# An f32 opening, later transfers of two key groups, and eight more probability chunks transposed by DMA, in an attention and routed feed-forward kernel

## The reference

```python
xn = layernorm(x)
q = xn @ W_qk                                   # keys are xn itself
scores = q @ xn.T / 16 + slope * (kpos - qpos)  # causal, softmax over keys
s = softmax(scores) @ (xn @ W_v.T)
probs = softmax(xn @ Wr); e = argmax(probs)     # 8 experts, 512 places each
h = relu(xe @ W1[e]); ye = (h @ W2[e]) * p      # tokens over capacity give 0
out = x + s * silu(ffn(xn))
```

## Time and profile before

| what | value |
|---|---|
| median of three runs | 441.39 us |
| profiled execution, whole | 440.56 us |
| its span, first to last instruction | 438.8 us |
| PE busy | 420.2 us (96%) |
| DVE busy | 323.6 us (74%) |
| ACT busy | 221.7 us (51%) |
| POOL busy | 231.0 us (53%) |
| granted TensorE clock | 1.0 throughout |

### The profile page before, as it was taken

One profiled execution on the slowest core, in us unless ns is written; L12 is line 12 of the kernel. 1 busy time (PEld: TensorE's weight loads), 2 busy tenths in 40 slices (PEclk: granted clock), 3 DMA queues, 4 the chain that ended last, 5 costly groups with the idle time before them and its releaser, 6 DMA issues.

```text
span 438.8 us, 8377 instructions
## 1 busy us (share of the span) xinstructions
PE 420.2 (96%) x3022; PEld 287.7 (66%) x3022; DVE 323.6 (74%) x839; ACT 221.7 (51%) x436; POOL 231.0 (53%) x360
## 2 busy tenths in 40 slices
PE   5799899997999899999999999999999999999996
PEld 2367576675678677676766666666666666665676
DVE  5989778988898568778758797979696966424563
ACT  1756365353655246645435554545454545454551
POOL 5337870834726735146202666575757575757530
PEclk9999999999999999999999999999999999999999
DMA  7992749465955643266746577676778773244850
GB/s 235 357 374 68 218 133 226 94 127 109 298 149 98 103 165 71 77 229 170 143 48 253 183 232 240 196 261 184 264 174 266 178 202 92 93 119 115 154 104 30
DMA packets 99928, 74.96 MB, mean 171 GB/s; under 512 B 68911, under 2 KB 93756, under 8 KB 97840
## 3 DMA queue, kind: packets, MB, share of 16 engines
q1 hardware_dynamic: 88624, 52.06, 45.6%
q0 software_dynamic: 5824, 16.74, 12.7%
q10 hardware_dynamic: 5440, 5.64, 4.0%
HBM read 31.33 MB, written 28.58 MB: 137 GB/s over the span
## 4 chain that ended last, share of the span: by engine, by line
PE 73%; DVE 13%; DMA 5%; ACT 4%; issue 3%; POOL 0%; another core or an unknown queue 0%; ACTq 0%; SPq 0%; DVEq 0%
PE bank L1350 19%; PE bank L1352 19%; PE bank L1351 19%; PE bank L1439 4%; PE bank L1442 4%; PE bank L1441 4%; DMA pT<-p_rows 4%; DVE sc L975 3%; PE bank L1420 3%; DVE p_rows L996 2%; ACT sc L1224 2%; DVE stats L823 1%; DMA xg<-in_x 1%; DVE pT L996 1%; DVE w_l L1047 1%
## 5 line engine op out<-in xcount | busy, mean ns | idle before, releaser
L1439 PE MATMUL bank<-v_h,pT 128*128 128x257 f16 x272 | 74.6, 274 | 3.3 <-DMA pT<-p_rows 3.2
L1442 PE MATMUL bank<-v_h,pT 128*128 128x257 f16 x272 | 74.1, 272 | 0.0
L1441 PE MATMUL bank<-v_l,pT 128*128 128x256 f16 x272 | 73.7, 271 | 0.0
L1251 ACT ACTIVATE hid_h<-bank 128x512 f16<-128x512 f32 x64 | 38.0, 594 | 67.2 <-PE bank L1352 61.3
L1065 DVE SCALAR_TENSOR_TENSOR hid_l<-bank,hid_h 128x512 f16<-128x512 f32 x64 | 43.9, 685 | 37.8 <-ACT hid_h L1251 35.4
L1351 PE MATMUL bank<-w_l,hid_h 128*128 128x256 f16 x256 | 69.8, 273 | 0.0
L1350 PE MATMUL bank<-w_h,hid_h 128*128 128x256 f16 x256 | 69.8, 273 | 0.0
L1352 PE MATMUL bank<-w_h,hid_l 128*128 128x256 f16 x256 | 69.8, 273 | 0.0
L975 DVE CUSTOM_DVE_ANT_0 sc<-bank,bias,score_mul 128x512 f32<-128x512 f32 (+2 forms) x80 | 52.9, 664 | 9.6 <-PE bank L1352 9.3
L1350 PE MATMUL bank<-xT,qT_h 128*128 128x512 f16 (+3 forms) x160 | 55.0, 347 | 2.7 <-DVE cmin L975 2.4
L1351 PE MATMUL bank<-xT,qT_h 128*128 128x512 f16 (+3 forms) x160 | 55.1, 347 | 0.0
(11 more groups left out here) (183 smaller groups left out, 917.1 us busy)
## 6 DMA issues: line engine op xcount, KB each, us to landing
raw<-in_w_e SPq DMA_DIRECT2D x5, 2048.0 KB
sc<-in_w_e SPq DMA_DIRECT2D x3, 2048.0 KB
slots<-empty ACTq DMA_DIRECT2D x1, 4224.0 KB, 20.1
gates<-gate SPq DMA_DIRECT2D x8, 512.0 KB
out<-xg SPq DMA_DIRECT2D x7, 512.0 KB
rows<-xg SPq DMA_DIRECT2D x7, 512.0 KB, 7.0
rows<-so SPq DMA_DIRECT2D x7, 512.0 KB
xg<-in_x SPq DMA_DIRECT2D x6, 512.0 KB, 4.9
```

Source lines behind the costliest of these rows:

```text
L1251: a_.activation(hid_h[:, f % HB, :], sc_ps[f % 2][:, :], ACT.Relu).then_inc(h_hi, 1)
L1439: pe.matmul(pv_ps[t % 2][:, 0:D + 1], p_h, v_h[:, at, q, 0:D + 1], start=kb == 0, stop=False)
L1441: pe.matmul(pv_ps[t % 2][:, 0:D], p_h, v_l[:, at, q, :], start=False, stop=False)
L1442: last = pe.matmul(pv_ps[t % 2][:, 0:D + 1], p_l, v_h[:, at, q, 0:D + 1], start=False, stop=kb == t % NT)
```

## The change

It has three parts. **The opening**: PE transposes the f32 rows of groups 0 and 1 (8 transposes a group, where 16 of f16 halves stood), and the halves are made from PSUM after it (`turned_high` on ACT, `turned_low` on DVE). The rows that `slots` needs are brought back by four DMA transposes for each of the two groups (`rows_of`). ACT takes roots and DVE refines them for group 0, ACT takes the statistics of two tiles of group 1; the clearing of `slots` is issued later on ACT, the first expert's weights at tile 5. **The key groups**: those of group 4 are requested after tile 11's chunks, those of group 5 after tile 15's. **The chunks**: every full chunk of tiles 20 to 23 (five), chunk 0 of tile 27 and chunks 0 and 1 of tile 31 join `by_dma`, 38 in place of 30. There are three row buffers, the third is a part of `hid_h`, and arrivals are counted for each chunk position.

```diff
-        p_rows = [sb(f"p_rows{k}", [P, GT, 2, P], F16) for k in range(2)]
+        p_rows = [sb(f"p_rows{k}", [P, GT, 2, P], F16) for k in range(NX - 1)]
+        p_rows += [hid_h[:, HB - 2:HB, :].rearrange("p f t -> p (f t)").rearrange("p (b h t) -> p b h t", b=GT, h=2)]
...
         def by_dma(t, c):
-            if t in (REST - 1, TILES - 1):
+            if chunk_blocks(t, c) < GT:
                 return False
-            if chunks(t) == 4:
-                return c == 1 if t == NT - 1 else c in ((1, 2) if t < NT else (0, 1, 2))
-            return chunks(t) == 3 and c < 2
+            if t < NT:
+                return c == 1 if t == NT - 1 else c in {3: (0, 1), 4: (1, 2)}.get(chunks(t), ())
+            return c in {REST - 1: (0,), TILES - 1: (0, 1)}.get(t, range(chunks(t)) if t >= NT + GT else ())
...
+        TURN_TILE = {2: 3, 3: 6, 4: 11, 5: 15, 6: 15, LATE: REST - 8}
...
+            def rows_of(g):
+                sp.wait_ge(xT_lo, 2 * g + 2)
+                for j in range(GT):
+                    sp.dma_start_transpose(halves[g][:, j, :].rearrange("p (b d) -> p b d", d=P),
+                                           xT[:, g, j, :, :].rearrange("p b t -> p (b t)")).then_inc(rows_back[g], 16)
...
-                    if i >= 2:
-                        act.wait_ge(pT_in[i % 2], i // 2 * 16)
+                    if dma_no(t, c) >= NX:
+                        b, m = in_rows[dma_no(t, c) - NX]
+                        act.wait_ge(pT_in[b % 2][m], landed(b, m))
...
+            def turned_low(g, h):
+                dve.wait_ge(xT_hi, 2 * g + h + 1)
+                hi, lo = tile_rows(g, h)
+                v.scalar_tensor_tensor(lo, turned_tiles(h), X_UP, hi, ALU.mult, ALU.subtract).then_inc(xT_lo, 1)
...
+            a_.activation(warm[:, 4:5], empty[:, 0:1], ACT.Sqrt)
+            roots(0)
+            mean(2)
+            square(2)
             act.wait_ge(small_scaled, 1)
             a_.activation(wqk_h[:, :, :], wsmall[:, 0], ACT.Copy, scale=small_up[:, 0:1]).then_inc(small_hi, 1)
-            split(0)
+            mean(3)
+            turned_high(0, 0)
+            turned_high(0, 1)
+            square(3)
+            act.dma_start(slots.rearrange("(k p) r -> p k r", p=P),
+                          empty[:, :].unsqueeze(1).to_broadcast([P, T // P, ROW])).then_inc(slots_empty, 16)
             small_highs()
+            roots(1)
             unit(0, QRY)
             unit(0, QRY + 1)
+            a_.activation(warm[:, 4:5], empty[:, 0:1], ACT.Exp)
...
                 for j in range(2):
+                    pe.wait_ge(xn_made, g * GT + 2 * h + j + 1)
+                    for d in range(KD):
+                        at = (j * KD + d) * P
+                        last = pe.transpose(x_ps[h][:, at:at + P], xn[:, 2 * h + j, d * P:(d + 1) * P], ident[:, :])
```

More of the change, by code:

```diff
@@ L227, in layer_kernel @@
         small_turn, small_back = bank[1][0:3, 0:P], bank[6][:, 0:3]
-        x_ps = [pv_ps[h][:, :].bitcast(F16) for h in range(2)]
+        x_ps = pv_ps
         w_turn, w_back = aux[0][0:2, 0:P], aux[1][:, 0:2]
@@ L273, in layer_kernel @@
         x_turned = sem("x_turned")
-        xT_front = sem("xT_front")
-        xT_rear = sem("xT_rear")
+        root_made = sem("root_made")
+        seed_made = sem("seed_made")
+        mean_made = sem("mean_made")
+        square_made = sem("square_made")
+        xT_hi = sem("xT_hi")
+        xT_lo = sem("xT_lo")
+        rows_back = [sem(f"rows_back{k}") for k in range(2)]
         xn_hi = sem("xn_hi")
@@ L296, in layer_kernel @@
         pT_lo = sem("pT_lo")
-        pT_in = [sem(f"pT_in{k}") for k in range(2)]
+        pT_in = [[sem(f"pT_in{k}_{c}") for c in range(NG)] for k in range(2)]
         pv_full = sem("pv_full")
@@ L367, in dma_no, with landed @@
             return chunk_no(t, c) - turn_no(t, c)
+        in_rows = [(t, c) for t in range(TILES) for c in range(chunks(t)) if by_dma(t, c)]
+        def landed(t, c):
+            return sum(by_dma(k, c) for k in range(t % 2, t + 1, 2)) * 16
         def chunk_cols(t, c):
@@ L448, in piece, with var_to, tile_rows, turned_tiles @@
             return q // PIECES, slice(q % PIECES * PIECE, (q % PIECES + 1) * PIECE)
[L450 to L457, removed]
+        def var_to(g):
+            return 1 if g == 0 else g + 2
+        def tile_rows(g, h):
+            return xT[:, g, 2 * h:2 * h + 2, 0:KD, :], xT[:, g, 2 * h:2 * h + 2, KD:2 * KD, :]
+        def turned_tiles(h):
+            return x_ps[h][:, :].rearrange("p (j k t) -> p j k t", j=2, k=KD)
+        def made_to(g):
+            return g * GT + GT if g < 2 else GT + GT + g - 1
+        def rows_to(g):
+            return g - 1
         def turned_to(g):
@@ L541, in _ @@
             group_in(0)
[L542 removed]
+            rows_of(0)
             for t in range(REST):
@@ L551, in _ @@
                         group_s(g - 1)
+                if t == 1:
+                    rows_of(1)
+                if t == 5:
+                    sp.dma_start(raw[:, :, :], w_k[0]).then_inc(w_in[1], 16)
                 if t == SPLIT_TILE[NG + 1]:
@@ L1076, in _ @@
             step(v.tensor_scalar(logit_mul[:, :], small_dn[:, 2:3], 1.0 / X_UP, None, ALU.mult))
+            dve.wait_ge(root_made, 2)
+            v.reciprocal(seed[1][:, :], root[:, :]).then_inc(seed_made, 1)
             value_weights()
             unit(0, QRY)
+            for j in range(GT):
+                normed(1, j)
             unit(0, QRY + 1)
-            for j in range(GT - 1):
-                normed(1, j)
-            split(1)
             unit(0, VAL)
+            turned_low(1, 0)
+            dve.wait_ge(masked, 1)
+            score(0, 0)
             unit(0, VAL + 1)
-            rear(1)
+            turned_low(1, 1)
             for n in range(VAL + 2, RANK):
@@ L1372, in unit @@
                     cols = slice((n - QRY) * P, (n - QRY + 1) * P)
-                    for d in range(KD):
-                        last = product(a[:, :], wqk_h[:, d, cols], wqk_l[:, d, cols],
-                                       xT[:, at, :, d, :], xT[:, at, :, KD + d, :], d == 0, d == KD - 1)
+                    for j in [slice(0, 2), slice(2, GT)] if g == 0 else [slice(0, GT)]:
+                        if g == 0 and j.start:
+                            pe.wait_ge(xT_lo, 2)
+                        for d in range(KD):
+                            last = product(a[:, j.start * P:j.stop * P], wqk_h[:, d, cols], wqk_l[:, d, cols],
+                                           xT[:, at, j, d, :], xT[:, at, j, KD + d, :], d == 0, d == KD - 1, True)
                 elif n < RANK:
@@ L1515, in _ @@
             unit(0, VAL)
-            score(0, 0)
-            unit(0, VAL + 1)
             turn_x(1, 0)
             turn_x(1, 1)
+            unit(0, VAL + 1)
+            score(0, 0)
             unit(0, VAL + 2)
```

214 lines of the change are left out of this document (110 added, 104 removed).

## The result

The changed kernel takes 453.19 us (median of four runs, 450.51 to 454.05) against 441.54 for the kernel before: 1.0254 times as long, 95% interval 1.0225 to 1.0282 (the two medians alone give 1.0264). That is 10.8 us over the forecast of 442.4 and outside its range. The profiled execution took 453.86 us, its span 451.8, which is 13.0 more than before.

The account below looks back on a forecast made before the run. PE bounds the kernel, busy 420.2 of 438.8 us. Terms -2.7 + 1.7 + 1.3 + 0.2 + 1.1 - 0.2 = +1.4 gave 442.0 from the profiled execution, 442.8 from the median; forecast 442.4, range 437.6 to 445.4.

Parts of the forecast that it names:

- Opening, -2.7: Start of kernel: first query product of group 1 at 22.25 us, where it stood at 24.98; bounds -3.2 and 0.
- The rival in which `slots` starves a load: Opening: the moved clearing delays group 2's x, statistics 3 to 4 us late, gain gone; near 445 us, chance 12%.
- Groups 4 and 5: Tiles 11 to 15: no wait at (11, 0), but `gate`, (15, 1) and group 5's keys late; +1.7 us, -1.2 to +3.0.
- The last link: After tile 15: group 5's `xT` lands at 151.6 to 152.9 us; PE wants it at 150.72 plus its own shift.
- Tiles 20 to 23: Five chunks by DMA: 0.3 lost at (20, 0), 3.1 us wait at (21, 0), five times 0.44 won; +1.3 us with DVE's lag.
- Second weights: Loaded behind (23, 1) at about 191 us; chunk (24, 0) moves behind 6 us of them; +0.2 us, 0 to +1.0.
- Chunk (27, 0): Behind the two loads of expert rows: 1.55 us lost waiting, 0.44 won; +1.1 us, bounds +0.6 and +2.5.
- the tail: Up to tile 31: two chunks less to turn win 0.88, PE waits 2.0 for (31, 0); -0.2 us, -1.0 to +0.8.
- The third buffer: In the tail: takes ACT's landing waits away; PE wins only 0.4 us from them and its 0.58 wait.
- The first rival: Tiles 10 to 23: late landings mostly absorbed, middle -1.2, tiles 20 to 23 +0.1; sum -3.1, near 438 us, chance 28%.

Follow-up runs that it names:

- weights first: The changed kernel with SP's issue of the second expert weights (2 MB) put ahead of tile 23's chunks; 449.86 us.
- the kernel without tiles 20 to 23: The changed kernel with the five full chunks of tiles 20 to 23 turned by PE again, not by DMA; 446.16 us.

## Why the prediction was wrong, step by step

The sum was +1.4, the profile has +13.0: -2.8 for the opening, +3.0 for groups 4 and 5, +1.2 for a pause of ACT, +4.4 for tiles 20 to 23, +5.6 for the second weights, +1.3 for (27, 0) and +0.3 for the tail.

**Opening, -2.7: right.** -2.76 at (0, 0), the first product of group 1 at 22.22 for a forecast of 22.25. The table switch cost 1.31, as the row said. By the rule of the Trainium skill ("ScalarE: Activation LUTs", "What ACT_TABLE_LOAD costs") it would have been about 2.66; the trace disagrees. The rival in which `slots` starves a load would have taken this gain away, and it was there.

**Groups 4 and 5, +1.7: right mechanism, too small.** The links up to tile 13 were there: (11, 0) without a wait, `tops` at 102.76 (104.97 less the 2.7 of the opening is 102.3), `gate` at 110.0, DVE idle 4.5 us, and tile 13's first transposes at 112.92 for 115.47, about the opening's shift, as forecast. From there DVE's delay reached PE sooner than forecast, in waits for scores (0.77 at 119.58, 0.48 at 123.11) and then at (15, 1), issued at 142.00 and landed after 5.0 where 3.1 to 4.5 was given. PE went from -2.76 to +0.24, +3.0, the upper bound. The last link did not come: PE, late already, never waited for group 5's `xT`. A further 1.16 came from the pause of ACT at 157 us: none of the other twelve profiles with the opening has it, so it belongs to that execution.

**Tiles 20 to 23, +1.3: the place right, the size wrong.** The wait at (21, 0) was there, 3.9 in place of 3.1. The half clock behind it, 1.7, stood in no term. The transposes of (23, 1), 0.44, won almost nothing: a wait of PE for DVE's `counts`, 0.69 at 190.06 in the kernel before, grew to 1.06. (The prediction had PE without a gap from 150 to 397 us, and missed this one.) Together +4.4.

**Second weights, +0.2: the step that failed.** It cost 5.6 us, the largest of all: a wait of 3.8 and 1.6 of half clock. I had them issued at 191, 2.6 us ahead of chunk (24, 0), gave them 6 us, and so took the chunk to land about when it was wanted; how the 0.2 follows, the prediction does not show. From the issue of the weights to the landing of the chunk it took 12.1 us, and 11.7 and 11.8 in two kernels more. Taking off PE's shift of 5.8, the weights go at 191.2 and the chunk lands at 203.3, wanted at 199.4: the wait of 3.8. What fills the 12.1 us is only in part shown: 2 MB and POOL's rows go through the engines first (393 GB/s at 201 us), then the engines are nearly idle for a microsecond (25 GB/s at 206), then the rest follows up to the landing. With the weights first, (23, 0) landed 9.0 after their issue; POOL's rows came only then, from 198.1. I counted the load's time, and not the chunk's behind it. The Trainium skill's rule on ring order ("DMA: Bandwidth & Descriptors", "Queues, rings and completion order"), which the prediction used for (21, 0), speaks for the same here, and the trace agrees at both places: 5.6 us from issue to landing behind the store, 9.7 behind the load. Whether it is the order on each engine or only the shared bandwidth, no run separates.

**Chunk (27, 0), +1.1, and the tail, -0.2: right in this kernel, by luck.** They measured +1.3 and +0.3. In the series that undoes the chunks one by one, (27, 0) cost 3.8 us of PE's shift, the tail 3.7 (4.9 against the tail without its two chunks), and each 3.9 by the medians. (27, 0) lands 3.2 to 3.6 us after its issue in all of them, but a PE that comes earlier waits 2.1 to 2.4 for it in place of 1.6; (31, 0) lands after 5.0 in place of 3.3. The clock falls behind (27, 0), and behind (31, 0) in three of four profiles.

**The clock had no term.** Every forecast wait was priced at its own length. In these profiles (PE's idle first 3.1 us of the program apart) a stretch at 0.50 came with each of the waits of 3.4 us and more, three of the four of 2.8 (not the 2.79 at (31, 0) of the kernel without tiles 20 to 23), and the 2.38 and 2.08 at (27, 0), but not the 2.37 at (23, 0), nor those under 2. Behind a wait at values it cost 1.6 to 1.7 us where the work compared is the same, and 2.5 where the clock had fallen before PE was back; 3.3 in the changed kernel's two places.

**The third buffer** was given 0.4 and, with the tail's chunks left on PE, was worth more than the forecast of the whole tail.

**The first rival's sum** does not come out either: with second weights and tail as above it is -2.7, not -3.1. It did not come about.

The theory that the loss is a row of late landings made by SP's order holds for the key groups, (21, 0), the weights and (27, 0), each by its own undoing. For tile 31's chunks their removal shows the cost, and why they land late stays open. With all of them undone, what is left of the change is faster than before, 438.38 and with (15, 1) moved 437.09.

## What to carry to other kernels

A transpose moved from a full engine to a DMA queue gains its 0.44 us only where it lands early; count what stands in front of it on the queue through to its landing, not to its issue, and take the time from issue to landing from a place with the same things ahead of it. Give a forecast wait of a nearly full PE a second price, for the clock that may fall behind it, 1.6 to 1.7 us here. And when one edit moves engines earlier, look at which fixed landing the next one will wait for.

## What the runs showed of the hardware that I had not expected

A DMA transpose of a chunk (256 KB) takes 3.3 us from issue to landing or 5.0, in the same place of nearly the same kernel, and 9.7 when 2 MB were issued 2.4 us ahead of it. A stretch at 1.2 GHz can follow an idle PE of 2.1 to 3.9 us. Behind values (21, 0) it began 0.7 us after PE was back at work and lasted 3.4; behind two waits of 3.5 us (group 4's keys, and (24, 0) without chunk (21, 0)) it was there when PE came back. It did not come where PE was kept busy with products that nobody reads.
